# Convolution tiles of 64 and 32 rows, a column sum on GpSimd, and a new order of loads and vector work, in a two-layer image kernel on one core

## What is computed

```
def haar2d(x):   a,b,c,d = the four phases of 2x2 pixels
    ll, lh, hl, hh = (a+b+c+d)/2, (a-b+c-d)/2, (a+b-c-d)/2, (a-b-c+d)/2
for i in range(3):                      # three wavelet levels
    co = haar2d(cur); cur = co[:, :, 0]
    coeffs[i] = dwconv5x5(co, wconv_w[i]) * wscale[i]
next_ll = 0
for i in reversed(range(3)):
    next_ll = ihaar2d(coeffs[i] with next_ll added to its ll band)
return x + dwconv5x5(xn, base_w) * base_scale + base_b + next_ll      # xn = group norm of x; cur starts as xn
```

## Time and profile before

| | us |
|---|---|
| median of 3 runs | 10908.44 |
| lowest and highest of them | 10892.28, 10910.33 |
| the profiled execution | 10874.65 |
| its span | 10872.8 |

### The profile page before, as it was taken

How to read it: one execution, slowest core, us unless ns; L and a number is a source line. 1 busy time by engine, 2 the same in 40 slices (tenths; PEclk the granted TensorE clock), 3 DMA queues, 4 the chain that set the end, 5 groups by cost and what they waited for, 6 DMA issues and landing times.

```text
span 10872.8 us, 205183 instructions
## 1 busy us (share of the span) xinstructions
PE 10462.5 (96%) x66084; PEld 8922.4 (82%) x66084; DVE 9149.1 (84%) x16540; ACT 7181.6 (66%) x11852; POOL 3711.4 (34%) x3719
## 2 busy tenths in 40 slices
PE   4999999999999999999799999999999999999999
PEld 4888888888888888888678888888888888888887
DVE  6999999899999989988777777777777777777777
ACT  4887878778787777788555555555555555555554
POOL 3444444444444444444322222222222222222222
PEclk9999999999999999999899999999999999999999
DMA  5433333333433324322277777777777777777775
GB/s 188 136 95 127 113 113 132 106 119 102 136 113 109 130 92 136 112 72 81 71 155 153 157 157 154 155 153 154 158 155 155 154 153 155 158 154 156 154 152 125
DMA packets 1162869, 1453.49 MB, mean 134 GB/s; under 512 B 215391, under 2 KB 1125023, under 8 KB 1125279
## 3 DMA queue, kind: packets, MB, share of 16 engines
q1 hardware_dynamic: 1161055, 1442.80, 52.6%
q10 hardware_dynamic: 1376, 6.13, 0.1%
HBM read 1040.11 MB, written 408.56 MB: 133 GB/s over the span
## 4 chain that ended last, share of the span: by engine, by line
PE 28%; DVE 17%; issue 4%; ACT 1%; DMA 0%; SPq 0%; POOL 0%; DVEq 0%; POOLq 0%
PE ps_w L1312 5%; PE ps_w L1313 5%; PE ps_w L1314 5%; PE ps_ll L1320 4%; DVE ob L1458 4%; DVE x L1389 3%; DVE zb L1402 2%; DVE zb L1405 1%; PE ps_w L1364 1%; PE ps L1352 1%; PE ps_w L1366 1%; DVE sum L1429 1%; PE ps L1312 1%; PE ps L1313 1%; PE ps L1314 1%
## 5 line engine op out<-in xcount | busy, mean ns | idle before, releaser
L1312 PE MATMUL ps_w<-zb,mat 128*128 128x512 f32 x4800 | 1925.6, 401 | 8.8
L1313 PE MATMUL ps_w<-zb,mat 128*128 128x512 f32 x4800 | 1906.2, 397 | 0.0
L1314 PE MATMUL ps_w<-zb,mat 128*128 128x512 f32 x4800 | 1905.2, 397 | 0.0
L1458 DVE SCALAR_TENSOR_TENSOR ob<-ps_w,prm,x 64x512 f32<-64x512 f32 x1920 | 1440.7, 750 | 516.0 <-PE ps_w L1364 477.2
L641 POOL CAST xn_hi<-xs 96x512 fp32r<-96x512 f32 x1024 | 878.3, 858 | 2918.0 <-PE ps_qkv L666 2087.0
L1263 ACT ACTIVATE z<-x,prm 64x384 f32<-64x384 f32 (+1 forms) x3072 | 1813.7, 662 | 58.7 <-DVE x L1389 51.0
L1205 POOL CAST mat<-raw 128x1280 fp32r<-128x1280 f32 (+1 forms) x288 | 469.5, 1648 | 3942.6 <-DMA raw<-vec 2350.0
L664 PE MATMUL ps_qkv<-wqkv_hi,xn_hi 96*128 96x288 f32 x4096 | 1387.2, 339 | 47.1 <-issue 22.3
L643 POOL TENSOR_TENSOR xn_lo<-xs,xn_hi 96x512 fp32r<-96x512 f32 x1024 | 1355.8, 1324 | 81.9
L666 PE MATMUL ps_qkv<-wqkv_hi,xn_lo 96*128 96x288 f32 x4096 | 1212.1, 296 | 0.0
L665 PE MATMUL ps_qkv<-wqkv_lo,xn_hi 96*128 96x288 f32 x4096 | 1209.9, 295 | 0.0
(11 more groups left out here) (202 smaller groups left out, 23976.0 us busy)
## 6 DMA issues: line engine op xcount, KB each, us to landing
xst<-in_x SPq DMA_DIRECT2D x96, 2048.0 KB, 14.1
xs<-in_x SPq DMA_DIRECT2D x128, 1536.0 KB, 9.0
y_scratch<-ys SPq DMA_DIRECT2D x128, 1536.0 KB, 9.6
out<-ob SPq DMA_DIRECT2D x768, 208.0 KB
xb<-in_x SPq DMA_DIRECT2D x576, 256.0 KB
yb<-y_scratch SPq DMA_DIRECT2D x576, 256.0 KB
raw<-vec SPq DMA_DIRECT2D x192, 320.0 KB, 4.3
raw<-vec SPq DMA_DIRECT2D x384, 160.0 KB, 4.0
```

The lines of the kernel that those rows point to most:

```text
L1312: mm(out_, w[HI], xx[HI], start=start, stop=False)
L1313: mm(out_, w[HI], xx[LO], start=False, stop=False)
L1314: return mm(out_, w[LO], xx[HI], start=False, stop=stop)
L1458: last = v.scalar_tensor_tensor(out=ob[p:p + WROWS, t // 2].rearrange("p b w -> p (b w)")[:, q::2], in0=ps_w[t][q * WROWS:(q + 1) * WROWS, ...
```

## The change

Four tiles of 64 rows stay, with less overlap (`TILES` gives start, rows skipped and rows of result: 60, 56, 56 and 60), and the fifth, `SPECIAL`, has 32 rows (24 of result) in **four** column phases of 64 columns. It has three column taps and matrices `mat_s` of its own: 9 matmuls of 256 columns in place of 15 of 512. Its z is `zq` and `zs`, its x1 is `x1_s`. Since its rows are spread over four phases, its part of `sum_down` needs a sum over column pairs first, which POOL makes once a group (`sum_columns`: a sum, a cast, a subtraction). ACT makes the normalised rows `zn` first, and `zq` out of them last; its copy of `ps_3` moves into the middle of `norm`, and `leading` behind `next_ll`'s high parts. DVE's order changes as shown below. The masks of the edge tiles go, only the pads are zeroed, and `down_sb` and `up_sb` are built on the chip.

```diff
-NV1 = 4 * TAPS * 2
+NV1 = 4 * (TAPS + 2) * 2
+SROWS = WROWS // 2
+SPHASES = 128 // SROWS
+STAPS = 3
+SPECIAL = WINDOWS - 1
@@ sync: load_raw has 8 more DMAs
+                    for ia in range(2):
+                        for q in range(SPHASES):
+                            first = q * SROWS + ia
+                            sp.dma_start(raw_s[first:first + SROWS - 1:2, :, :],
...
@@ sync: group
                         load(m3 * 2 + k3, g3)
                         if g == 0 and more:
                             load_gain(m * 2 + (k + 2), k)
+                    if g == 0 and (more or k == 0):
+                        sp.wait_ge(mat23_ready, m * 2 + (k + 1))
+                        load_raw(m * 2 + (k + 1))
                     store(m * 2 + k, g, m * 4 + (2 * k + g))
-                sp.wait_ge(zeroed, N_ZERO)
...
                         load_prm(m * 2 + (k + 2), k)
-                        sp.wait_ge(mat23_ready, m * 2 + (k + 2))
-                        load_raw(m * 2 + (k + 2))
@@ gpsimd
+                def sum_columns(qn, done, count, first=False):
+                    pool.wait_ge(done, count)
+                    pool.wait_ge(zn_set, qn + 1)
+                    if not first:
+                        pool.wait_ge(ll_ready, qn)
...
+                def channel(c, k):
+                    sum_columns(c * 2 + 1, mat23_ready, c + 1)
+                    build_first(c + 1, 1 - k)
+                    sum_columns(c * 2 + 2, mat1_ready, c + 2)
+                    build_levels(c + 1)
@@ scalar: norm and steps
+                    for b in range(IMGS):
+                        img = IMGS * g + b
+                        last = nc.scalar.activation(
+                            zn[:, b], x1_s[own(k, g), b], ACT.Identity,
...
+                    last.then_inc(zn_set, 1)
                     for p in range(2):
+                        if p == 1 and between is not None:
+                            between()
...
+                    act.wait_ge(zn_set, m * 4 + (2 * k + g + 1))
+                    for q in range(SPHASES):
+                        last = nc.scalar.activation(zq[q * SROWS:(q + 1) * SROWS].rearrange("p b j -> p (b j)"),
+                                                    rows_and_sums[SROWS:2 * SROWS, q::SPHASES], ACT.Copy)
                     last.then_inc(z_set, 1)
@@ tensor: sum_down and conv
+                    for t in range(SPECIAL):
+                        pe.wait_ge(z_lo, qn * WINDOWS + (t + 1))
...
+                    pe.wait_ge(ls_lo, qn + 1)
+                    for h in (HI, LO):
+                        last = mm(ps_ll[:], down_sb[0:SROWS, SPECIAL, :], ls_hl[h][:], start=False, stop=h == LO)
...
+                        if t == SPECIAL:
+                            for d in range(STAPS):
+                                split(ps_w[t][:, 0:IMGS * BLOCKS], [mat_s[k][h][:, d, :] for h in range(2)],
+                                      [zs[g][h][:, :, d:d + BLOCKS] for h in range(2)], d == 0, False)
+                            return
@@ vector: steps
                     if before:
-                        finish(qn - 1, mb, kb, gb_, (0,))
+                        finish(qn - 1, mb, kb, gb_, (0, 1))
                     make_in(qn)
                     if before:
-                        finish(qn - 1, mb, kb, gb_, (1,))
+                        finish(qn - 1, mb, kb, gb_, (2,))
                     split_in(qn)
                     if before:
-                        finish(qn - 1, mb, kb, gb_, range(2, WINDOWS))
+                        finish(qn - 1, mb, kb, gb_, (3, 4))
+                    up_levels(qn)
+                    split_next(qn)
+                    if n is None or n + 1 < GROUPS_C:
+                        trailing(qn + 1, ahead(m, k, g, 1)[2])
                     if n is None or n + 2 < GROUPS_C:
                         make_x1(*ahead(m, k, g, 2))
-                    if n is None or n + 1 < GROUPS_C:
-                        trailing(qn + 1, ahead(m, k, g, 1)[2])
-                    up_levels(qn)
-                    split_next(qn)
```

More of the change, by code:

```diff
@@ L1039, in wt_attention_kernel @@
             mat1 = [[sbr_(f"mat1_{k}_{h}", [128, TAPS, 2 * WROWS]) for h in range(2)] for k in range(2)]
+            mat_s = [[sbr_(f"mat_s{k}_{h}", [128, STAPS, 128]) for h in range(2)] for k in range(2)]
             mat2 = [sbr_(f"mat2_{h}", [128, 2, TAPS, HALF]) for h in range(2)]
@@ new lines, in build_first @@
+                def build_first(c, k, first=False):
+                    pool.wait_ge(raw_in, c * NRAW + NRAW)
+                    if not first:
+                        pool.wait_ge(out_ready, c * (2 * WINDOWS) + (LEAD - 2 * WINDOWS))
+                    pool.sem_inc(pool_turn, 1)
+                    build([(mat1[k], raw1[:].rearrange("p (d o) m -> p d (o m)", o=2)[:, :, ::-1], "p d m -> p d m"),
+                           (mat_s[k], raw_s[:].rearrange("p (d o) m -> p d (o m)", o=SPHASES)[:, :, ::-1],
+                            "p d m -> p d m")],
+                          mat1_hi, mat1_ready, c + 1)
@@ new lines, in build_levels @@
+                def build_levels(c):
+                    pool.wait_ge(l2_ready, c * 2 + 1)
+                    pool.sem_inc(pool_turn, 1)
+                    build([(mat2, raw2[:, :, ::-1], "p s d m -> p (s d) m"),
+                           (mat3, raw3[:, :, ::-1], "p s d m -> p (s d) m")],
+                          mat23_hi, mat23_ready, c + 1)
+                def channel(c, k):
[3 more added lines that the diff above has]
+                    build_levels(c + 1)
@@ L1231, in loop_groups @@
+                sum_columns(0, zeroed, N_ZERO, True)
+                build_first(0, 0, True)
+                build_levels(0)
+                with pool.Fori(0, C // 2 - 1) as m:
+                    for k in range(2):
+                        channel(m * 2 + k, k)
+                channel(C - 2, 0)
+                sum_columns(C * 2 - 1, mat23_ready, C)
             def loop_groups(eng, steps):
@@ L1456, in finish @@
                                 dve.wait_ge(prm_in[k], mc * 16 + 16)
-                        for q in range(2):
+                        for q in range(SPHASES if t == SPECIAL else 0):
+                            last = v.scalar_tensor_tensor(
+                                out=ob[0:SROWS, t // 2].rearrange("p b w -> p (b w)")[:, q::SPHASES],
+                                in0=ps_w[t][q * SROWS:(q + 1) * SROWS, 0:IMGS * BLOCKS], scalar=prm[k][own(k, g), 1:2],
+                                in1=x1_s[own(k, g)].rearrange("p b w -> p (b w)")[:, q::SPHASES],
+                                op0=ALU.add, op1=ALU.add)
+                        for q in range(0 if t == SPECIAL else 2):
                             last = v.scalar_tensor_tensor(
```

228 lines of the change are left out of this document (128 added, 100 removed).

## The result

The changed kernel takes **11675.0 us** (median of 4 runs, 11671.79 to 11676.75) against 10909.39 us of the kernel before (4 runs in the same job, 10892.28 to 10911.56): ratio **1.0705**, interval 1.0687 to 1.0724, slower. The prediction said 11610, in 11030 to 11850. The profiled execution is 11674.04 us, with a mean granted clock of 0.945 (0.991 before).

The account below looks back on a forecast made before the run. PE bounds the kernel before; a once-a-channel loop through SP, POOL, PE, ACT and DVE was to replace it, 63.9 us against 56.3. Over 95 channels 722 us more, less 10 at the start: 11610 us, range 11030 to 11850.

Parts of the forecast that it names:

- The loop: Once a channel: x1's end, loads and raw DMAs, POOL's building and column sum, PE's sum_down, x1 again; 63.9 us against 56.3.
- B: SP and DMA, from x1's end until ten loads and 18 raw DMAs are issued and the raw matrices landed: 22.4 us.
- C: POOL's build_first of mat1 and mat_s, 4.3 us alone plus 4.0 for taking turns with DVE's trailing and x1: 8.3 us.
- A: From PE's start of tile 0 of an even group, through ACT and DVE, to the end of x1(2c+2): 29.2 us.
- D: POOL's sum_columns for the next channel's first group (sum, cast, subtraction and gaps): 3.5 us.
- E: PE's last two matmuls of sum_down, at the end of the turn: 0.5 us.
- x1's instructions are 1.8 long: On DVE in odd groups: x1's instructions, all 1.27 us before, would be some 1.8 long.
- The start: Kernel start, where SP no longer waits for 17 us of zeroing: 10 us gained (0 to 15).
- rival 1: The loop as laid, once a channel, with POOL and DVE colliding: 11250 to 11850 us; chance 0.62.
- Rival 2: The loop without POOL and DVE colliding, 57.8 us a channel: 11040 us; chance 0.20.
- Rival 3: PE stays the bound because raw matrices land before POOL must build, 25.2 us a group: 10340 us; chance 0.13.
- Rival 4: PE's clock falls after its long hole, tiles 0 and 1 taking up to 14 us, not 7: 11900 us; chance 0.05.

Follow-up runs that it names:

- e5_raw_s_once: Changed kernel, with the eight raw_s DMAs of the special tile issued for channel 0 only: 11487.46 us, ratio 1.0488 to the kernel before.
- e9_gated: Changed kernel with x1 early, sum_columns ahead of build_first, and POOL's mat2 and mat3 subtractions waiting for trailing: 10489.71 us, ratio 0.9577 to the kernel before.
- e1_raw_first: Changed kernel, with the next channel's raw DMAs issued ahead of the wait for x1 and the ten loads: 11356.39 us, ratio 1.0414 to the kernel before.
- e8_warm: Changed kernel, with 30 extra matmuls of unread result in PE's hole ahead of the wait for ls: 11808.33 us, ratio 1.0787 to the kernel before.
- e2_x1_early: Changed kernel, with DVE making x1 behind the finish of tiles 3 and 4, ahead of up_levels: 10848.71 us, ratio 0.9946 to the kernel before.
- e6_before_x1_last: Kernel before, with only x1 moved to the end of DVE's step: 11084.16 us, ratio 1.0119 to the unedited kernel before.
- e7_before_raw_next: Kernel before, with only the raw DMAs moved: the next channel's, behind the loads of a channel's first group: 10808.43 us, ratio 0.9866.
- e11_not_gated: Changed kernel with x1 early and sum_columns ahead of build_first, POOL's subtractions not waiting for trailing: 10703.58 us, ratio 0.9774 to the kernel before.

## Why the prediction was right, step by step

The loop was right at each step. That its sum came within 1 us is in part luck: B was 3.0 too small and C 2.4 too large. In us:

| term | predicted | measured | |
|---|---|---|---|
| A | 29.2 | 28.6 | 8044.10 to 8072.67 |
| B | 22.4 | 25.4 | 8008.12 to 8033.53 |
| C | 8.3 | 5.9, gap 0.3 | 8033.53 to 8039.39 |
| D | 3.5 | 3.2 | 8039.67 to 8042.90 |
| E | 0.5 | 1.2 | to tile 0 at 8044.10 |
| sum | 63.9 | 64.6 | |

- **A**: near, though parts were off. PE came to level 3 at +9.7 and not at +7.05, because of the half clock (0.50 from 8040 to 8048 us), and the matrices were ready at +9.6 (predicted +11.1). So the wait for them of "near 4" us a channel is not there: 4.7 us in all of the 4000. `zq` is 2.65 for four (0.66 each, not 0.535).
- **B, mis-sized**: the eight raw_s DMAs take 6.54 us of SP's queue, 0.82 each, where I took 0.5 each, 4.0. That is 2.5 of the 3.0. The ten loads and the gain took 7.4 (8008.35 to 8015.77) against 6.8, the old ten raw DMAs with their gaps 7.8 against 7.6, and from the end of the last raw issue (8030.33) to POOL's first cast it was 3.2 against 4.0; two gaps of 0.2 remain. SP issued all the raw DMAs in 14.4 us, not in 11 to 12.
- **C, mis-sized by B**: I laid the landing 20 us behind the start of the odd group's tile 0 and on `trailing` and x1 whole. It came later, with most of that done, so POOL lost 1.6 us (casts 2.81 for 1.24) and not 4.0. "x1's instructions are 1.8 long" was wrong: only `x_s` was held, 1.62 for 1.27. e5_raw_s_once shows the two coupled: when B falls by 4.7, C and D rise by 2.7.
- The first cast, started at 8033.53, lasts 1.31 us for 0.72 and ends 0.6 us behind x1's second instruction (8034.27); the second lasts 1.50 for 0.52 and ends 0.4 behind `x_s` (8035.92). The Trainium skill, "SBUF — State Buffer", section "Who interferes with whom", says that a Vector instruction with two SBUF inputs and a GpSimd instruction that reads SBUF contend. These rows agree. What was off was the time at which they meet.
- PE stands still for 9.8 us a channel (500.0 and 106.6 us in 62 channels), not 14. Its own work is about 52 us, not 50, and the half clock adds 3.2 (2.7 in tiles 0 and 1, 0.5 ahead of them); together 65.
- **D** as predicted, **E** 1.2 for 0.5, by the clock.
- **The start**: the first `sum_down` begins at 5446.06, against 5455.76, 9.7 us gained where I said 10.
- The total: (64.8 - 56.3) x 95 - 10 = 798, and the profiled executions differ by 799.39. The sum's 63.9 gives 722 - 10; the 0.2 between this turn and the mean period is in no term.
- The upper bound of rival 1 was added up too low: 63.9, 1.1 and 1.5 are 66.5 before "more contention", not 66, so 11870 and above the stated range. Nothing measured hangs on it.

Rival 1 won. Rival 2 (no collisions, 11040) fell with B and C: 25.4 in place of 22.4 alone takes its 57.8 to 60.8. Rival 3 (PE stays the bound) is far off in the changed kernel, but its mechanism is what e9_gated does; its 10340 (25.2 us a group) was 150 us too low, since PE's group there is 25.9 us or more and not 25.0. Of these 0.9 us, 0.6 are in up-sampling and `sum_down`, which the prediction kept at 3.8 for 16 matmuls; in e9_gated these 17 take 4.4, at full clock and without a wait, from the first row to the second:

```profile
8040.72 0.72 PE L1455 MATMUL ps_w<-next_a,up_sb 128*128 128x512 f32 x2
...
8045.09 0.50 PE L1392 MATMUL ps_w<-zb,mat 128*128 128x512 f32 x1
```

Rival 4 saw the half clock and that PE's wait for `mat2` hides part of it. It took tiles 0 and 1 at up to 14 us; they take 9.7, and the late level matrices hide all of that.

What the prediction did not see is the wait behind the loop. Had the raw matrices come in time, its rival 3 would have promised a gain, and e1_raw_first, where they do, takes 61.4 us a channel: with x1 last, PE waits at tile 0 of every group.

## What to carry to other kernels

Moving work to the end of an engine's step isn't free because it isn't urgent: look at what stands behind it (here the next tile's `finish`) and at the wait that it used to fill. When a wait is queued ahead of a product that the bound engine needs (`build_first` ahead of `sum_columns`), write down the loop, and after cutting it look for the next one before counting the gain. A gate on the engine whose product is not needed yet was worth 2.2 us a channel here, but read what it moved: the instructions that it was meant to free were not the ones that became shorter.

## What the runs showed of the hardware

- The granted clock fell behind short holes too, but not behind each: in e8_warm PE stood still for 2.77 us behind busy time at full clock, and the windows from 8036 to 8044 us were granted 0.57; in e2_x1_early holes of 0.9, 0.4 and 0.9 us between 8024 and 8029 are followed by a window (8028 to 8032) at 0.64. In e6_before_x1_last holes of 1.25 and 1.42 us end at 8028.52 and 8034.01, and all windows from 8024 to 8040 have 1.00. In the changed kernel the windows from 8040 to 8048, at and behind the end of an 8.3 us hole, were granted 0.50.
- A raw_s DMA of 16 x 12 pieces of 128 bytes takes 0.82 us of SP's queue, a raw1 DMA of 32 x 10 pieces of 256 bytes only 0.74: neither pieces nor bytes alone give the price. What stands ahead in the queue counts too: the two raw2 DMAs take 1.49 us behind the raw_s ones in the changed kernel, and right behind the raw1 ones 1.35 in the kernel before, 2.94 in e5_raw_s_once and 3.86 in e7_before_raw_next; the eight raw_s ones take 5.98 in e1_raw_first.
- Four DVE subtractions of 128x512 take 2.50 us alone, 4.5 us beside POOL's subtractions (e11_not_gated) and 6.13 beside its casts and subtractions (e2_x1_early).
